# Scores from split operands in three fp32r passes, squares on GpSimd, all raw copies on ScalarE

## What is computed

```
q = (x @ Wq).reshape(B, T, H, D)
k = (x @ Wk).reshape(B, T, H, D)
v = (x @ Wv).reshape(B, T, H, D)
q = _rmsnorm(q, q_rms_w)
k = _rmsnorm(k, k_rms_w)
...
gate_logits = jnp.einsum('bthd,hd->bht', k, u_n) / math.sqrt(D)
gate = jax.nn.softplus(gate_logits)
...
bias = -dist[None, None] * omega_eff[None, :, None, None] * gate[:, :, None, :]
bias = jnp.where(causal[None, None], bias, -jnp.inf)
scores = jnp.einsum('bihd,bjhd->bhij', q, k) * scale + bias
attn = jax.nn.softmax(scores, axis=-1)
y = jnp.einsum('bhij,bjhd->bihd', attn, v).reshape(B, T, H * D)
return y @ Wproj
```

## Time and profile before

| | us |
|---|---|
| runs: median (lowest, highest), 3 runs | 1401.46 (1395.56, 1401.74) |
| the profiled execution | 1394.83 |
| its span | 1393.1 |
| TensorE matmuls busy | 1338.3 |
| TensorE weight loads busy | 1087.9 |
| VectorE busy | 1030.8 |
| ScalarE busy | 905.6 |
| GpSimd busy | 199.4 |
| mean granted TensorE clock | 0.982 |

### The profile page before, as it was taken

How to read it: one execution, slowest core, us unless ns; L and a number is a source line. 1 busy time by engine, 2 the same in 40 slices (tenths; PEclk the granted TensorE clock), 3 DMA queues, 4 the chain that set the end, 5 groups by cost and what they waited for, 6 DMA issues and landing times.

```text
span 1393.1 us, 28875 instructions
## 1 busy us (share of the span) xinstructions
PE 1338.3 (96%) x9936; PEld 1087.9 (78%) x9936; DVE 1030.8 (74%) x3228; ACT 905.6 (65%) x2294; POOL 199.4 (14%) x564
## 2 busy tenths in 40 slices
PE   4779999999999999999999999999999799999998
PEld 3567778777877878787778778777877589899997
DVE  6939996889698778868896887888688665554442
ACT  5748785878588677858885886778588533333333
POOL 4602111111111111101111111111011100000000
PEclk8879999999999999999999999999999899999999
DMA  6532232232223322322423232323232221111100
GB/s 215 193 114 93 96 100 85 85 114 92 99 71 107 97 76 94 100 85 85 134 72 99 71 125 79 97 73 105 80 92 93 78 69 43 43 42 43 43 16 31
DMA packets 88322, 122.95 MB, mean 88 GB/s; under 512 B 8577, under 2 KB 74482, under 8 KB 88178
## 3 DMA queue, kind: packets, MB, share of 16 engines
q1 hardware_dynamic: 87858, 121.11, 27.2%
q10 hardware_dynamic: 320, 0.00, 0.0%
HBM read 101.69 MB, written 19.40 MB: 87 GB/s over the span
## 4 chain that ended last, share of the span: by engine, by line
PE 90%; DVE 2%; ACT 1%; issue 1%; DMA 0%; SPq 0%; POOL 0%; DVEq 0%; ACTq 0%; POOLq 0%
PE at L814 19%; PE at L892 11%; PE at L865 10%; PE at L823 10%; PE at L1510 7%; PE at L936 7%; PE at L1546 7%; PE at L846 3%; PE at L828 3%; PE at L920 2%; PE at L903 2%; PE at L857 2%; PE at L851 2%; PE at L1529 1%; PE at L1476 1%; PE at L1540 1%
## 5 line engine op out<-in xcount | busy, mean ns | idle before, releaser
L1065 ACT ACTIVATE prob<-prob,low 128x512 f32<-128x512 f32 (+3 forms) x512 | 280.6, 550 | 118.1 <-DVE low L1205 118.1
L1205 DVE CUSTOM_DVE_ANT_0 prob<-at,mask 128x512 f32<-128x512 f32 (+3 forms) x512 | 220.1, 485 | 39.9 <-PE at L828 39.9
L814 PE MATMUL at<-w_hi,c_lo 128*128 128x386 f32 x512 | 190.8, 373 | 6.5 <-DVE area_raw L1154 5.7
L823 PE MATMUL at<-kT,qT 64*128 64x512 f32 (+3 forms) x1024 | 184.6, 441 | 5.4 <-ACT kaug L1056 3.5
L1218 DVE TENSOR_SCALAR prob<-prob,rec 128x512 f32<-128x512 f32 (+3 forms) x512 | 172.7, 401 | 4.5
L814 PE MATMUL at<-w_lo,c_hi 128*128 128x386 f32 x512 | 175.2, 342 | 0.0
L814 PE MATMUL at<-w_hi,c_hi 128*128 128x386 f32 x512 | 174.9, 342 | 0.0
L865 PE MATMUL at<-ident,prob 128*128 128x128 f32 x1280 | 165.7, 277 | 2.4 <-DVE prob L1218 1.4
L892 PE MATMUL at<-probT,v 128*64 128x512 f32 (+3 forms) x1024 | 153.6, 442 | 3.4 <-DVE probT L1228 2.6
L865 PEld LDWEIGHTS at<-ident,prob 128*128 128x128 f32 x1280 | 143.5, 142 | 10.1 <-DVE yT_lo L1234 1.6
L828 PE MATMUL at<-kaug,qaug 64*128 64x512 f32 (+3 forms) x512 | 141.5, 547 | 0.0
(11 more groups left out here) (220 smaller groups left out, 2887.0 us busy)
## 6 DMA issues: line engine op xcount, KB each, us to landing
area_w<-in_L_ffn_w SPq DMA_DIRECT2D x65, 1024.0 KB, 5.6
bias<-in_L_ffn_w SPq DMA_DIRECT2D x160, 32.0 KB, 4.6
x_in<-in_L_attn_x SPq DMA_DIRECT2D x8, 512.0 KB, 6.2
xr<-in_L_attn_x SPq DMA_DIRECT2D x8, 512.0 KB, 5.0
eo_d<-eo SPq DMA_DIRECT2D x32, 128.0 KB, 1.8
x_d<-xr SPq DMA_DIRECT2D x8, 512.0 KB, 2.9
area_raw<-x_d SPq DMA_DIRECT2D x8, 512.0 KB, 4.0
out<-area_raw SPq DMA_DIRECT2D x8, 512.0 KB, 3.0
```

What stands on the lines that cost most here:

```text
L814: m = eng.matmul(bQ[n % 2][:, 0:W], a[:, (j // HP) % 2, k, n * P:(n + 1) * P], w[:, k, j % HP, :], start=start, stop=(k == KC - 1 and a is ...
L823: eng.matmul(bC[i][:, at:at + (c + 1) * P], qT[rows, c * P:(c + 1) * P], kT[rows, 0:(c + 1) * P], start=True, stop=False)
L1065: eng.activation(sl, sl, ACT.Exp, scale=-1.0, bias=low[:, i:i + 1], accum_out=den[:, i:i + 1]).then_inc(exp_done.sem, 1)
L1205: eng.tensor_tensor_reduce(out=prob[s % 2][h][:, off[c]:off[c + 1]], in0=bC[i][:, at:at + (c + 1) * P], in1=mask[:, (NT - 1 - c) * P:T], s ...
```

## The change

- q and k are no longer kept as fp32 tiles. After the transposes ScalarE writes `qT_hi` (scaled) and `kT_hi` in fp32r (`copy_q`, `copy_k`), and VectorE the differences `qT_lo` and `kT_lo` (`low_q`, `low_k`), in the place behind `copy_y` and ahead of `divide(s, 1)`. The scores are summed from three fp32r products, hi with hi, lo with hi and hi with lo, and the bias. Of chunk 3, the first, each product has a wait of its own; before, all operands were waited for ahead of the scores.
- The square of the raw q and k goes from ScalarE to GpSimd, as a product of the tile with itself, at the head of GpSimd's turn. `take_v` goes behind `augment`.
- ScalarE copies the first raw piece too; VectorE's `take_raw` is gone.
- v has two buffers instead of three, `eo` lies in the memory of `hidT`, and `copy_hidden` waits for the store of the last `eo`.

```diff
-        qT = sb("qT", [P, T])
-        kT = sb("kT", [P, T])
+        qT_hi, qT_lo = sb("qT_hi", [P, T], F32R), sb("qT_lo", [P, T], F32R)
+        kT_hi, kT_lo = sb("kT_hi", [P, T], F32R), sb("kT_lo", [P, T], F32R)
...
-                ("probT0", [P, off[NT]], F32), ("probT1", [P, off[NT]], F32), ("v", [P, 3, NT, P], F32)),
-            (("hT_hi", [P, HC, T], F32R), ("hT_lo", [P, HC, T], F32R), ("mem", [P, T], F32)))
+                ("probT0", [P, off[NT]], F32), ("probT1", [P, off[NT]], F32), ("v", [P, 2, NT, P], F32)),
+            (("mem", [P, T], F32), ("hT_hi", [P, HC, T], F32R), ("hT_lo", [P, HC, T], F32R)))
...
-        eo = sb("eo", [P, C])
+        eo = hidT[:, :, :].rearrange("p f q -> p (f q)")
...
-                        eng.wait_ge(raw_A.sem, raw_A.at(j - 1, 2))
-                    elif n == 1:
                         eng.wait_ge(raw_A.sem, raw_A.at(j - 1, 3))
-                    elif n == 2:
-                        eng.wait_ge(raw_D.sem, raw_D.at(j))
                     else:
-                        eng.wait_ge(raw_A.sem, raw_A.at(j, 1))
+                        eng.wait_ge(raw_A.sem, raw_A.at(j, n - 1) if n > 1 else raw_A.at(j - 1))
...
-                def scores(c):
-                    for h in range(2):
-                        i, at = place[c, h]
-                        rows = slice(h * D, (h + 1) * D)
-                        eng.matmul(bC[i][:, at:at + (c + 1) * P], qT[rows, c * P:(c + 1) * P], kT[rows, 0:(c + 1) * P],
-                                   start=True, stop=False)
-                    for h in range(2):
-                        i, at = place[c, h]
-                        rows = slice(h * D, (h + 1) * D)
-                        m = eng.matmul(bC[i][:, at:at + (c + 1) * P], qaug[rows, c * P:(c + 1) * P],
-                                       kaug[rows, 0:(c + 1) * P], start=False, stop=True)
-                        m.then_inc(pe_s.sem, 1)
+                def scores(s, c):
+                    for q, k, ready in ((qT_hi, kT_hi, k_hi_done), (qT_lo, kT_hi, q_lo_done), (qT_hi, kT_lo, k_lo_done),
+                                        (qaug, kaug, kaug_done)):
+                        if c == NT - 1:
+                            eng.wait_ge(ready.sem, ready.at(s))
+                        for h in range(2):
+                            i, at = place[c, h]
+                            rows = slice(h * D, (h + 1) * D)
+                            m = eng.matmul(bC[i][:, at:at + (c + 1) * P], q[rows, c * P:(c + 1) * P], k[rows, 0:(c + 1) * P],
+                                           start=ready is k_hi_done, stop=q is qaug)
+                            if q is qaug:
+                                m.then_inc(pe_s.sem, 1)
...
+                    eng.wait_ge(q_hi_done.sem, q_hi_done.at(s))
                     for c in (3, 1, 2, 0):
-                        scores(c)
+                        scores(s, c)
...
-                            m = eng.matmul(bY[h * D:(h + 1) * D, kc * P:T], v[:, s % 3, kc, h * D:(h + 1) * D],
+                            m = eng.matmul(bY[h * D:(h + 1) * D, kc * P:T], v[:, s % 2, kc, h * D:(h + 1) * D],
...
-                        eng.wait_ge(raw_A.sem, raw_A.at(b * HP + HP + 2, n + 2))
+                        eng.wait_ge(raw_A.sem, raw_A.at(b * HP + HP + 2, n + 3))
...
-                        eng.wait_ge(qT_done.sem, qT_done.at(s))
-                        eng.wait_ge(kT_done.sem, kT_done.at(s))
-                        eng.wait_ge(kaug_done.sem, kaug_done.at(s))
                         all_scores(s)
...
                 def take_raw(j, n):
                     eng.wait_ge(pe_q.sem, pe_q.at(j, n + 1))
-                    if n == 1:
+                    if n == 0:
                         eng.wait_ge(v_done.sem, v_done.at(j - 2))
+                        eng.wait_ge(squared.sem, squared.at(j - 2))
                         eng.wait_ge(norm_done.sem, norm_done.at(j - 2))
                         eng.wait_ge(gate_in.sem, gate_in.at(j - 2))
                     eng.activation(raw[:, j % 2, n, :], bQ[n % 2][:, 0:W], ACT.Copy).then_inc(raw_A.sem, 1)
-
-                def square(j):
-                    eng.wait_ge(raw_A.sem, raw_A.at(j))
-                    eng.wait_ge(raw_D.sem, raw_D.at(j))
-                    eng.wait_ge(ssd.sem, ssd.at(j - 1, 1))
-                    eng.wait_ge(pe_t.sem, pe_t.at(j - 1, 2))
-                    eng.activation(sq[:, :, :], raw[:, j % 2, :, 0:2 * P], ACT.Square).then_inc(squared.sem, 1)
...
+                def copy_q(j):
+                    eng.wait_ge(pe_s.sem, pe_s.at(j - 1))
+                    eng.wait_ge(pe_t.sem, pe_t.at(j, 1))
+                    eng.activation(qT_hi[:, :], bR[0][:, :], ACT.Copy, scale=q_scale[:, 0:1]).then_inc(q_hi_done.sem, 1)
+
                 def copy_k(j):
-                    eng.wait_ge(pe_s.sem, pe_s.at(j - 1))
                     eng.wait_ge(pe_t.sem, pe_t.at(j, 2))
-                    eng.activation(kT[:, :], bR[1][:, :], ACT.Copy).then_inc(kT_done.sem, 1)
+                    eng.activation(kT_hi[:, :], bR[1][:, :], ACT.Copy).then_inc(k_hi_done.sem, 1)
...
                 for s in range(NTURN + 1):
-                    if s + 1 < NTURN:
-                        square(s + 1)
...
@@ -1113,6 +1104,7 @@
                     if s + 1 < NTURN:
                         rsqrt(s + 1)
                     if s + 2 < NTURN:
+                        take_raw(s + 2, 0)
                         take_raw(s + 2, 1)
...
                     if s + 1 < NTURN:
+                        copy_q(s + 1)
                         copy_k(s + 1)
                         copy_aug(s + 1)
...
-                def take_raw(j):
-                    eng.wait_ge(pe_q.sem, pe_q.at(j, 1))
-                    eng.wait_ge(v_done.sem, v_done.at(j - 2))
-                    eng.wait_ge(squared.sem, squared.at(j - 2))
-                    eng.tensor_copy(raw[:, j % 2, 0, :], bQ[0][:, 0:W]).then_inc(raw_D.sem, 1)
...
-                def copy_q(j):
-                    eng.wait_ge(pe_s.sem, pe_s.at(j - 1))
-                    eng.wait_ge(pe_t.sem, pe_t.at(j, 1))
-                    eng.tensor_scalar(qT[:, :], bR[0][:, :], q_scale[:, 0:1], None, ALU.mult).then_inc(qT_done.sem, 1)
+                def low_q(j):
+                    eng.wait_ge(q_hi_done.sem, q_hi_done.at(j))
+                    eng.scalar_tensor_tensor(qT_lo[:, :], bR[0][:, :], q_scale[:, 0:1], qT_hi[:, :].bitcast(F32), ALU.mult,
+                                             ALU.subtract).then_inc(q_lo_done.sem, 1)
+
+                def low_k(j):
+                    eng.wait_ge(k_hi_done.sem, k_hi_done.at(j))
+                    eng.tensor_tensor(kT_lo[:, :], bR[1][:, :], kT_hi[:, :].bitcast(F32), ALU.subtract).then_inc(k_lo_done.sem, 1)
...
                 def copy_hidden(m):
                     eng.wait_ge(pe_hT.sem, pe_hT.at(m))
-                    eng.wait_ge(pe_eo.sem, pe_eo.at(m - 1))
+                    eng.wait_ge(eo_store.sem, eo_store.at(m - 1))
                     eng.tensor_copy(hidT[:, :, :], bH[:, 0:FW].rearrange("p (f q) -> p f q", f=NF)).then_inc(hidT_done.sem, 1)
 
                 def copy_expert_output(m):
                     eng.wait_ge(pe_eo.sem, pe_eo.at(m))
-                    eng.wait_ge(eo_store.sem, eo_store.at(m - 1))
                     eng.wait_ge(bias2_load.sem, bias2_load.at(m))
-                    eng.tensor_tensor(eo[:, :], bX[:, 0:C], bias2[:, :], ALU.add).then_inc(eo_done.sem, 1)
+                    eng.tensor_tensor(eo, bX[:, 0:C], bias2[:, :], ALU.add).then_inc(eo_done.sem, 1)
...
-                take_raw(1)
-                copy_q(0)
+                low_q(0)
+                low_k(0)
...
@@ -1288,8 +1277,6 @@
                     if s < NTURN:
                         lows(s, 2)
                         lows(s, 0)
-                    if s + 2 < NTURN:
-                        take_raw(s + 2)
...
                     prepare(s, 2)
                     if ends_in(s) is not None:
                         copy_expert_output(ends_in(s))
-                    if s + 1 < NTURN:
-                        copy_q(s + 1)
                     if s > 0:
                         copy_y(s - 1)
+                    if s + 1 < NTURN:
+                        low_q(s + 1)
+                        low_k(s + 1)
                     if s < NTURN:
                         divide(s, 1)
                     prepare(s, 3)
...
+                def square(j):
+                    eng.wait_ge(raw_A.sem, raw_A.at(j))
+                    eng.wait_ge(ssd.sem, ssd.at(j - 1, 1))
+                    eng.wait_ge(pe_t.sem, pe_t.at(j - 1, 2))
+                    eng.tensor_tensor(sq[:, :, :], raw[:, j % 2, :, 0:2 * P], raw[:, j % 2, :, 0:2 * P], ALU.mult).then_inc(squared.sem, 1)
+
                 def take_v(j):
                     eng.wait_ge(raw_A.sem, raw_A.at(j))
-                    eng.wait_ge(raw_D.sem, raw_D.at(j))
-                    eng.wait_ge(pe_y.sem, pe_y.at(j - 3))
```

(8 more changed lines are left out.)

16 lines of the change are left out of this document (8 added, 8 removed).

## The result

The changed kernel takes 1461.13 us (median of four runs, 1460.43 to 1462.19), the kernel before in the same comparison 1398.88 us (four runs, 1395.56 to 1401.74). The ratio is 1.046, with a 95% interval of 1.043 to 1.049: the change makes the kernel slower. The forecast was 1497 us with a range of 1445 to 1530. The profiled execution of the changed kernel took 1460.54 us, that of the kernel before 1394.83: 65.7 us more, where the sum of the prediction came to 99.

What follows compares the result with a forecast made beforehand. TensorE was taken to bound the kernel, with 90% of the chain. Terms 87.5 + 6 + 9 + 2 - 3 - 2.5 gave +99 on 1394.83 us, 1494, put at 1497 with 3 us for run spread; range 1445 to 1530.

Steps and rivals of the forecast that it cites:

- The side and the mechanism: Slower: GpSimd's square holds VectorE's second multiplication of divide, delaying TensorE's transposes and projections by 1.59 us a turn.
- The square's duration: GpSimd's square of the raw q and k, 128x1024, was taken to last 2.4 us.
- Rival B: VectorE is held, but GpSimd's square takes only 1.35 us: +35 us, 1430; chance 0.06.
- How many turns: Attention-loop turns that lose: 63 boundaries, less 7 with output projection, less the last: 55, together 87.5 us.
- The saving of the scores: TensorE's score matmuls, four passes instead of five, save 0.34 us a turn, bounded by 0.22 and 0.54.
- Rival D: Splitting the scores saves nothing because weight loads limit all passes; changes nine turns only, 3 us; no separate chance given.
- Values waiting on ScalarE: ScalarE's later exponentials and extra raw copy delay the products with v: 0.25 us in 24 turns, 6 us.
- Behind gelu: Every fourth turn, late q and k copies get the first multiplication held too: 0.6 us in 15 turns, 9 us.
- copies cost nothing: Moving raw and q copies between ScalarE and VectorE costs nothing by itself; neither total changes over 0.2 us a turn.
- wp_lo: In turns 1 and 2 GpSimd computes wp_lo ahead of the square: 2 us more.
- The waits for the bias operand: TensorE's waits for the bias operand of the scores, now wanted only after three passes, end: 2.5 us gained.
- Rival A: GpSimd's square and VectorE's multiplications run side by side, so not slower: 24 us gained, 1371; chance 0.11.

Runs made afterwards that it cites:

- E3: Changed kernel with one wait more, so GpSimd's square starts only when the four multiplications of divide are over: 1387.8 us.
- E9: Changed kernel with the four multiplications of divide reading an idle PSUM bank instead of SBUF, in 54 of the 55 held turns: 1399.6 us.
- E4: Changed kernel with GpSimd's square written as two instructions of half the size, one after the other: 1457.8 us.
- E8: Changed kernel with divide(s, 1) placed ahead of low_q and low_k on VectorE: 1450.5 us.
- E2: Kernel before the change with only the square moved to GpSimd, at the head of its turn, v behind it: 1405.6 us.
- E5: Changed kernel with divide's last four multiplications reading one row and writing it as three: 1460.5 us.

## Why the prediction was right, and where it was off

**The side and the mechanism** were right. The order that it rested on (first multiplication, square, second multiplication) is in the trace to 0.02 us, E3 shows that the collision is the whole loss, E9 that it catches multiplications whose source is in SBUF.

**The square's duration** was the term that was mis-sized, and it makes most of the miss. I took 2.4 us from two rows with two different inputs; a tile times itself took 1.91. The view of this one line in the changed kernel (shortest, median, longest, in ns):

```profile
L1339 POOL TENSOR_TENSOR area_sq<-area_raw x64: 1895/1911/2011, 84.3 to 1136.1; 128x1024 f32<-128x1024 f32 x64
```

Per held turn that gives 1.10 instead of 1.59, over 54 turns 59 us instead of 87.5. Rival B had the right direction (both inputs are one tensor) and overdid it with 1.35; the rate of a copy was a poor bound. The truth lay near the middle, and I had given weight to the rows with the same number of inputs only. That the one tensor is the reason is not shown: the operations of the earlier trace rows are also differences and write fp32r, the square is a product and writes fp32, and no run separates these. That 1461 lies in the range is owed to its lower part, which was there for rival B; the middle was 36 us too high.

**How many turns**: 55 forecast. Of the 56 waits on `low`, two remain in E3, where nothing is held, so 54 turns lose: 2 to 62 without the seven behind an output projection. Turn 1, which I had counted in, takes 14.07 us and is not held.

**The saving of the scores**: 0.34 forecast, about 0.25 measured (turn 41 against before: -0.24; E3's plain turn: -0.24), inside the bounds of 0.22 and 0.54. The passes of the 128-column chunk start 0.06, 0.12 and 0.11 apart (715.67 to 715.96 above), and where nothing is held the chunk takes 0.49 us (turn 41), as the four loads had it and not the 0.34 of no limit. The three larger chunks take 1.03, 0.47 and 0.70 us (713.47, 714.50, 714.97, 715.67) instead of 0.98, 0.43 and 0.66: the excess of fp32r, which I left out of the middle value. All four take 2.70 us, before 2.95. Rival D, a split that saves nothing, is excluded by the same figures.

**Values waiting on ScalarE**: 6 us forecast, none seen: plain turns lost 1.09 us, which is what the later first projection matmul (S + 5.10 instead of S + 4.01) gives alone. With a shorter square ScalarE has 0.5 us more, and it needed 0.25.

**Behind gelu**: 0.6 more forecast, 0.48 measured (1.58 - 1.10 in turn 39), for the reason given: the first multiplication is held, and two more stand behind the square. But "copies cost nothing" was too kind there: once the square is out of the way, E3 shows the late copies as a cost, 14.79 against 14.50.

**wp_lo**: 2 us forecast. Turns 2 and 3 lost 1.17 and 1.25 us, where other turns with and behind gelu lost 1.14 and 1.57: nothing came on top.

Added up from the turns, the 54 held ones lose 66.0 us (59 at 1.10 each, 7 more behind gelu) and the nine others gain 2.2: 63.8, where the forecast had 87.5 + 6 + 9 + 2 - 3 - 2.5 = 99. The waits for the bias operand that are gone and the new ones for kT_hi, 5.0 us in 17, lie inside these lengths of turns. The remaining 1.9 us lie outside the loop and were not followed.

**Rival A** was rightly put low, but its price was wrong: with nothing held the kernel takes 1388 (E3) and not 1371. 0.25 instead of 0.34 a turn takes 6 us of it, the turns behind gelu, which grow by 0.29 instead of shrinking by 0.25, another 8, and the 2.5 for the bias operand are not gained on top. The row that was held for it was also misread. It said that neither the multiplication nor the copy of v beside it is longer, but the copy's 0.67 us is: at its new place in the changed kernel it takes 0.61 (median of 64). And the kernel before already had the collision, behind each gelu, where GpSimd copies v:

```profile
706.63 0.75 POOL L1351 COPY v<-area_raw 128x512 f32<-128x512 f32 x1 [3.62 <-ACT area_raw L1026]
```

```profile
706.83 0.63 DVE L1218 TENSOR_SCALAR prob<-prob,rec 128x128 f32<-128x128 f32 x1
```

Fifteen multiplications of 128x128 took 0.63 us there instead of 0.28. These rows would have put rival A lower than 0.11.

## What to carry to other kernels

Before moving work to GpSimd, look at which VectorE instructions from SBUF to SBUF come while it would run: a multiplication that came later than GpSimd's square waited for the whole instruction, and all that was queued behind it waited too, while instructions that read PSUM, and a small reciprocal, did not. Here it was cheaper to order the two than to shorten one: one wait more on GpSimd's side turned 1461 us into 1388, half the square 1461 into 1415. And where a term of a sum is a duration, take it from a row with the same operation, operands and types, not just the same number of inputs.

## What the runs showed of the hardware

- A GpSimd product of 128x1024 fp32 elements took 1.91 us when both inputs were one tile (1.89 in E3, where no multiplication runs at its start), where differences of two tiles, written in fp32r, took 2.18 and 2.55. The half took 1.06, so by an estimate about 0.2 us don't depend on the size (2 x 1.06 - 1.91).
- The hold is per GpSimd instruction, and is passed to and fro: in E4 GpSimd's second half ran its normal 1.03 us with a VectorE multiplication let out just ahead of it and another held behind it.
- VectorE instructions that read PSUM ran beside GpSimd at full speed: `lows` of 512 columns at 0.69 us (E3), low_q at 0.75 (E8), multiplications at 0.34 (E9).
- GpSimd waits as well: in E2 a square that began at 715.17, while a multiplication begun at 715.03 still ran, took 2.02 us instead of 1.89.
- One kind of VectorE instruction from SBUF to SBUF was not held: a reciprocal of 128x4 took its usual 0.17 us inside GpSimd's `wp_lo` (twice in the changed kernel, 1.94 and 1.79 us behind its start).
- Writing touching rows as three instead of one did not change a multiplication's 0.42 us (E5).
